# A spill store moved from ScalarE's program to SyncE's, in an attention stage that transposes its probabilities through HBM

## The chip, the core and the metric

The program runs on one core of one Trainium2 chip. The metric is the device time of one execution, in microseconds (us). The profiled execution is looked at through its span, from the first to the last instruction. PE is TensorE, PEld its weight loads, DVE is VectorE, ACT is ScalarE, POOL is GpSimd, SP is SyncE, which only issues DMAs here.

## The reference

Four layers follow one another on 2 x 1024 tokens of 256 features: attention with 16 heads of 128, a gated MLP, attention with 16 heads of 16, and a mixture of experts. The change lies in the first attention:

```python
q = x @ wq + bq; k = x @ wk + bk; v = x @ wv + bv          # weights are codes * scales
scores = einsum('bqhd,bkhd->bhqk', q, k) / sqrt(128)       # 2 batches, 16 heads, 1024 x 1024
attn = softmax(scores, axis=-1)
out = einsum('bhqk,bkhd->bqhd', attn, v).reshape(B, S, 2048)
return out @ wo + bo
```

## The kernel before

The first attention (attention0_stage) works in 8 passes of two heads each, numbered m = 0 to 7. A pass has 32 tiles (TILES): 2 batches x 2 heads x 8 tiles of 128 queries, each against all 1024 keys. Passes 1 to 6 are one hardware loop. Four tiles make a group (GT = 4), so a pass has 8 groups, numbered 0 to 7, with tiles 0 to 3 in group 0. Products are made in three passes of split float32 (line 81).

One tile goes through these steps:

- PE: score(m, tile), 6 matmuls into two of four PSUM banks. It waits until the exponential of tile - 2 is done.
- DVE: row_max (line 1060), the negated maximum of each row.
- ACT: exp (line 934) into one of two buffers prob. It waits for the maximum, and for the turned tile - 2.
- DVE: turn_prob (line 1066), a 32 x 32 block transpose into one of two buffers turned_prob. It waits until the store of tile - 2 has landed (the semaphores stored, four of them in turn).
- A store (line 940) of 512 KB to one of 8 slots of spill in HBM. ACT issues it once the tile is turned.
- A fetch (line 666) of 512 KB back into probT_lo, with 1 KB pieces that complete the transpose. SP issues it once the store has landed. The first fetch of a group also waits until group - 2 has been weighed, since there are two group buffers.
- ACT: probT_take (line 948), the high half. For the first tile of a group it waits for all four fetches of the group.
- POOL: split_lo (line 582), the low half.
- PE: weigh, 6 matmuls with v; then every group's result goes through wo (output) and is added up by DVE.

Each engine walks through slots, one per tile. In slot t PE makes the scores of tile t + 1, then a projection or output, then weighs tile t - 7. DVE in slot t turns tile t, takes the maximum of tile t + 1, then takes projections and outputs out of PSUM, in this order. ACT in slot t takes the high half of tile t - 6, a projection, issues the store of tile t and makes the exponential of tile t + 1:

```python
                if unit is not None and there(m, unit, QK):
                    take_qk(m, unit)
                if there(m, at, TILES):
                    store(m, at)
                if there(m, at + 1, TILES):
                    exp(m, at + 1)
```

SP runs exchange(m): for each group four fetches, and after some groups the loads of the next pass's weights (LOAD_AFTER: after group 0 the q weights and the biases, eight DMAs in lines 617, 621, 634 and 636; after group 1 k, after group 2 v, after group 5 o, five DMAs each). In pass 0, after group 1, set_acc (line 642) comes before the k weights: eight DMAs of 128 KB that each copy the one row bo to all partitions. In pass 7 no weights are loaded; after group 4 SP loads x again (2 x 512 KB) and the first weights of the MLP (lines 1165 to 1170).

DMAs of SP are queue q1 of the profile, those of ACT are queue q10.

Of the kernel before, what the change touches and what calls it, by code (L numbers as in the profile page):

```python
# [20 lines left out]
GT = NB // P  # L21
# [383 lines left out]
def attention0_stage(nc, k, name, ins, after, mlp):  # L405
# [8 lines left out]
    TILES, GROUPS, PARTS = BATCH * half_tiles, BATCH * half_tiles // GT, BATCH * half_tiles  # L414
# [21 lines left out]
    def there(m, i, per_pass):  # L436

        return not isinstance(m, int) or 0 <= m * per_pass + i < passes * per_pass

    def wait(eng, sem, m, per_pass, count):  # L440

        value = m * per_pass + count
        if not isinstance(value, int) or value > 0:
            eng.wait_ge(sem, value)
# [60 lines left out]
    with ExitStack() as ctx:  # L505
# [105 lines left out]
        def _(sp):  # L611
# [32 lines left out]
            def next_weights(m, what):  # L644
# [12 lines left out]
                else:  # L657
                    wait(sp, wo_ready, m, 2, 2)
                    load_wo(m + 1, landed_o)

            def fetch(m, tile):
                group = m * GROUPS + tile // GT
                if tile % GT == 0:
                    wait(sp, weighed, group - 1, GT, 0)
                sp.wait_ge(stored[tile % STORES], (group + 1) * 16)
                sp.dma_start(probT_lo[:, tile // GT % 2, :, tile % GT, :, :].bitcast(F32).rearrange("p a k n -> p a (k n)"),
                             spill[tile % SLOTS].rearrange("(a i) (b n) -> (i b) a n", a=NSQ, b=NSQ)).then_inc(fetched[tile // GT % 2], 16)

            def exchange(m):
                for group in range(GROUPS):  # L670
                    tiles = range(group * GT, (group + 1) * GT)
                    for t in tiles:
                        fetch(m, t)
                    if first(m) and group == 1:
                        for g in range(QG, norm.groups):
                            set_acc(g)
                    if not last(m) and group in LOAD_AFTER:
                        next_weights(m, LOAD_AFTER[group])
                    if last(m) and group == 4:
                        sp.wait_ge(wo_ready, 2 * passes)  # L680
                        for g in range(after.ahead):
                            after.load_x(sp, g)
                        mlp.load_first(sp)
                        mlp.load_second(sp)
# [236 lines left out]
        @block.scalar  # L921
        def _(act):
            def take_qk(m, unit):
                b, head, which, c = qk_part(m, unit)
                wait(act, qk_full, m, QK, unit + 1)
                to = (q, key)[which][0][:, head, c * NB:(c + 1) * NB]
                nc.scalar.activation(to, ring_bank(m, "qk", unit), ACT.Identity,
                                     bias=bias_qk[:, which * HP + head:which * HP + head + 1]).then_inc(qk_hi_done, 1)

            def exp(m, tile):  # L930
                wait(act, max_ready, m, TILES, tile + 1)
                wait(act, turned, m, TILES, tile - 1)
                by_key = scores(tile).rearrange("p a (n b) -> p b (a n)", b=NSQ)
                nc.scalar.activation(prob[:, tile % 2, :].rearrange("p (b n) -> p b n", b=NSQ), by_key, ACT.Exp,  # L934
                                     bias=neg_max[:, tile % 2:tile % 2 + 1],
                                     accum_out=total[:, tile % half_tiles:tile % half_tiles + 1]).then_inc(exp_done, 1)

            def store(m, tile):
                wait(act, turned, m, TILES, tile + 1)
                act.dma_start(spill[tile % SLOTS], turned_prob[:, tile % 2, :]).then_inc(stored[tile % STORES], 16)  # L940

            def probT_take(m, part):
                group, j = part // GT, part % GT
                if j == 0:
                    wait(act, fetched[group % 2], m, 16 * TILES // 2, 16 * GT * (group // 2 + 1))
                wait(act, weighed, m, PARTS, part - GT + 1)
                hi, lo = part_pair(part)
                nc.scalar.activation(hi, f32(lo), ACT.Copy).then_inc(hi_done, 1)  # L948

            def keep_o(m, group):  # L950
                wait(act, weighed, m, PARTS, (group + 1) * GT)
                wait(act, out_full, m, OUTS, 2 * group)
                nc.scalar.activation(o[0][:], o_bank(group), ACT.Copy).then_inc(o_hi_done, 1)

            def v_hi(m, piece):
                half, head = piece // 4, piece // 2 % 2
                wait(act, v_taken, m, V, 4 * half + 2 * (piece % 2 + 1))
                wait(act, weighed, m, PARTS, 16 * half - 8 * (1 - head))
                to, cols = v_piece(piece)
                nc.scalar.activation(v[0][:, to, cols], v_whole[:, to, cols], ACT.Copy).then_inc(v_hi_done, 1)  # L960

            def weights(m, at):
                if not last(m):
                    if at in QK_HI:
                        head = QK_HI[at]
                        wait(act, multiplied, m, 4, 2 if head == 0 else 3)
                        wait(act, qk_full, m, QK, 8 + 4 * (head + 1))
                        nc.scalar.activation(by_row(w[0][:, 0:2, :, head_cols(head)]), by_row(qk_codes[:, :, :, head_cols(head)]),
                                             ACT.Copy).then_inc(w_hi_done, 1)
                    if at == V_HI:  # L970
                        wait(act, multiplied, m, 4, 3)
                        wait(act, v_full, m, V, V)
                        nc.scalar.activation(flat(w[0])[:, 2 * nq:WQKV], codes[:, 2 * nq:WQKV], ACT.Copy).then_inc(w_hi_done, 1)
                if not first(m) and at in WO_HI:
                    head = WO_HI[at]
                    wait(act, multiplied, m, 4, 0)
                    wait(act, out_full, m, OUTS, 0 if head else -4)
                    nc.scalar.activation(wo[0][:, head, :], codes[:, wo_cols(head)], ACT.Copy).then_inc(wo_hi_done, 1)

            def slot(m, at):  # L980
                part = at + 1 - WEIGH_AT
                if there(m, part, PARTS):
                    probT_take(m, part)
                if (at - KEEP_AT) % GT == 0 and there(m, (at - KEEP_AT) // GT, GROUPS):
                    keep_o(m, (at - KEEP_AT) // GT)
                if first(m) and at in TAKE_AT:
                    g = TAKE_AT[at]
                    act.wait_ge(norm.turned, g + 1)
                    norm.take_hi(act, g, turn_banks(g))
                unit = qk_unit(at)  # L990
                if unit is not None and there(m, unit, QK):
                    take_qk(m, unit)
                if there(m, at, TILES):
                    store(m, at)
                if there(m, at + 1, TILES):
                    exp(m, at + 1)
                piece = v_split_at(m, at)
                if piece is not None and there(m, piece, V_PIECES):
                    v_hi(m, piece)
                if at < TILES:  # L1000
                    weights(m, at)
                if last(m):
                    if at in NORM_ACC:
                        after.early_scalar(act, NORM_ACC[at])
                    if at in NORM_X:
                        after.normalise_x(act, NORM_X[at])
                    if at == FIRST_HI:
                        nc.scalar.activation(neg_max[:, 0:1], neg_max[:, 0:1], ACT.Silu)
                        mlp.first_hi(act, first_scaled, first_hi)
                    if at in TAKE_X:  # L1010
                        g = TAKE_X[at]
                        act.wait_ge(after.turned, g + 1)
                        after.take_hi(act, g, last_turn_banks(g))

            for g in range(QG):
                norm.normalise_x(act, g)
            for g in range(QG):
                norm.take_turned(act, g)
            for unit in range(4):
                take_qk(0, unit)  # L1020
                if unit == 1:
                    for g in range(QG, norm.groups):
                        norm.normalise_x(act, g)
            each_slot(act, slot)
# [1645 lines left out]
```

## Time and profile before

| | |
|---|---|
| three runs | 2025.73, 2030.62, 2036.57 us |
| median | 2030.62 us |
| the profiled execution's own time | 2030.62 us |
| its span | 2028.9 us |
| mean granted TensorE clock | 0.97 |
| PE busy over the span | 1906.4 us (94%) |
| PE weight loads, DVE, ACT, POOL busy | 1500.5, 1444.7, 1180.0, 1150.0 us |
| last instruction of the first attention, about | 1157 us |

Busy times of engines overlap, so they don't add up to the span. Each time in a timeline is the start of an instruction from the span's start. The time to landing of a DMA runs from its issue to its completion. A wait is put down to what ended it. Idle time of an engine that is not the bottleneck costs nothing.

### The profile page before, as it was taken

The page shows a single profiled execution, that of the slowest core. Times are in us where ns is not written, and L with a number is a line of the kernel's source. Part 1 is how long each engine was busy: PE and PEld are TensorE (multiplying, and loading weights), DVE is VectorE, ACT ScalarE, POOL GpSimd, SP SyncE. Part 2 cuts the span into 40 slices and gives each one's busy share as a digit, 9 for nine tenths or more (in the row PEclk, how much of TensorE's full clock was granted, in tenths as well). Part 3 has the DMA queues.
Part 4 walks back from the last instruction along what each step waited for, and adds up shares of the span by engine and source line. Part 5 has one row for each costly group of instructions (what it writes and reads, how often), then busy time and mean ns, then how long its engine had stood idle before and what let it go on. Part 6 is the DMA issues. An engine that isn't in the chain of part 4 may idle for free. (4 is left out here: it accounts for less than half of the span.)

```text
span 2028.9 us, 31398 instructions
## 1 busy us (share of the span) xinstructions
PE 1906.4 (94%) x10632; PEld 1500.5 (74%) x10632; DVE 1444.7 (71%) x2367; ACT 1180.0 (58%) x1939; POOL 1150.0 (57%) x856
## 2 busy tenths in 40 slices
PE   6899999999999999999998799899999898999996
PEld 4688888888888888888887587645554457788885
DVE  5678878888788878888888654587677736455555
ACT  4566666666666666666666554377667654333333
POOL 2576776777767767777666562134343435344443
PEclk8899999999999999999999899999999979899998
DMA  7877877878778777787778310000000010110001
GB/s 157 266 249 262 289 258 257 272 261 275 249 257 289 257 254 271 264 269 250 263 254 279 114 43 1 9 7 4 4 4 1 1 56 24 32 32 24 16 1 42
DMA packets 211794, 310.29 MB, mean 153 GB/s; under 512 B 16368, under 2 KB 174832, under 8 KB 211696
## 3 DMA queue, kind: packets, MB, share of 16 engines
q1 hardware_dynamic: 174832, 174.77, 29.7%
q10 hardware_dynamic: 36864, 134.23, 16.4%
q8 instruction: 59, 0.97, 0.2%
q14 instruction: 39, 0.32, 0.1%
HBM read 172.64 MB, written 136.31 MB: 152 GB/s over the span
## 5 line engine op out<-in xcount | busy, mean ns | idle before, releaser
L582 POOL TENSOR_TENSOR attn_probT_lo<-attn_probT_lo,attn_probT_hi 128x1024 fp32r<-128x1024 f32 x254 | 609.7, 2402 | 198.5 <-ACT attn_probT_hi L948 197.9
L1066 DVE STREAM_TRANSPOSE attn_turned_prob<-attn_prob 128x1024 f32<-128x1024 f32 x256 | 318.0, 1242 | 108.0 <-ACT attn_prob L934 58.9
L934 ACT ACTIVATE attn_prob<-psum,attn_neg_max 128x1024 f32<-128x1024 f32 x256 | 285.5, 1115 | 145.9 <-DVE attn_neg_max L1060 143.7
L1060 DVE TENSOR_REDUCE attn_neg_max<-psum 128x1 f32<-128x1024 f32 x256 | 305.7, 1194 | 30.9 <-PE psum L81 30.9
L948 ACT ACTIVATE attn_probT_hi<-attn_probT_lo 128x1024 fp32r<-128x1024 f32 x256 | 269.5, 1053 | 22.8 <-DMA attn_probT_lo<-attn_spill 22.8
L81 PE MATMUL psum<-attn_probT_hi,attn_v_hi 128*128 128x512 f32 x512 | 209.2, 409 | 20.4 <-POOL attn_probT_lo L582 18.7
L81 PE MATMUL psum<-attn_key_hi,attn_q_hi 128*128 128x512 f32 x512 | 204.3, 399 | 7.1 <-ACT attn_prob L934 3.9
L81 PE MATMUL psum<-attn_probT_hi,attn_v_lo 128*128 128x512 f32 x512 | 207.2, 405 | 0.0
L81 PE MATMUL psum<-attn_probT_lo,attn_v_hi 128*128 128x512 f32 x512 | 206.0, 402 | 0.0
L81 PE MATMUL psum<-attn_key_hi,attn_q_lo 128*128 128x512 f32 x512 | 203.2, 397 | 0.0
L2425 ACT ACTIVATE attn_probT<-psum 128x512 f32<-128x512 f32 (+3 forms) x384 | 163.1, 495 | 66.6 <-PE psum L2310 60.0
L81 PE MATMUL psum<-attn_key_lo,attn_q_hi 128*128 128x512 f32 x512 | 200.6, 392 | 0.0
L1624 POOL TENSOR_TENSOR attn_qk_lo<-attn_moe_hidden,attn_qk_hi 128x512 fp32r<-128x512 f32 x72 | 94.3, 1310 | 182.4 <-ACT attn_qk_hi L1588 182.4
L1988 DVE TENSOR_REDUCE attn_peaks<-psum 128x1 f32<-128x512 f32 (+1 forms) x256 | 155.9, 651 | 39.8 <-PE psum L1959 26.3
L785 POOL TENSOR_TENSOR attn_v_lo<-attn_v_whole,attn_v_hi 128x512 fp32r<-128x512 f32 x64 | 83.1, 1299 | 127.9 <-ACT attn_v_hi L960 127.9
L1651 DVE TENSOR_TENSOR attn_moe_hidden<-psum,attn_v 128x512 f32<-128x512 f32 x72 | 49.7, 690 | 137.6 <-ACT attn_v L1582 103.9
L81 PEld LDWEIGHTS psum<-attn_probT_hi,attn_v_hi 128*128 128x128 f32 x512 | 96.9, 189 | 44.1 <-POOL attn_probT_lo L582 12.4
L81 PE MATMUL psum<-xT_hi,attn_q 128*128 128x512 f32 x288 | 119.6, 415 | 6.6 <-POOL attn_key L1620 6.5
L81 PE MATMUL psum<-xT_hi,attn_w_hi 128*128 128x512 f32 x288 | 116.5, 405 | 6.6 <-POOL attn_bias_v L726 5.6
L81 PEld LDWEIGHTS psum<-attn_key_hi,attn_q_hi 128*128 128x128 f32 x512 | 96.8, 189 | 31.8 <-ACT attn_prob L934 5.2
L81 PE MATMUL psum<-xT_hi,attn_key 128*128 128x512 f32 x288 | 117.6, 408 | 0.0
L1588 ACT ACTIVATE attn_qk_hi<-attn_moe_hidden 128x512 fp32r<-128x512 f32 x72 | 45.5, 633 | 123.9 <-DVE attn_moe_hidden L1651 123.9
(237 smaller groups left out, 4782.3 us busy)
## 6 DMA issues: line engine op xcount, KB each, us to landing
attn_spill<-attn_turned_prob ACTq DMA_DIRECT2D x256, 512.0 KB, 3.9
attn_probT_lo<-attn_spill SPq DMA_DIRECT2D x256, 512.0 KB, 5.4
attn_v_all<-in_moe_w SPq DMA_DIRECT2D x23, 384.0 KB, 3.0
acc_sb<-in_x SPq DMA_DIRECT2D x4, 512.0 KB, 7.7
x_sb<-in_wq_codes SPq DMA_DIRECT2D x8, 256.0 KB, 3.9
x_sb<-in_wq_scales SPq DMA_DIRECT2D x32, 64.0 KB, 4.0
x_sb<-in_wk_codes SPq DMA_DIRECT2D x8, 256.0 KB, 4.2
x_sb<-in_wk_scales SPq DMA_DIRECT2D x32, 64.0 KB, 4.9
```

The lines of the kernel that those rows point to most:

```text
L81: ins = nc.tensor.matmul(out, stationary[s], moving[m], start=start and n == 0, stop=stop and n == len(PASSES) - 1)
L582: engine.tensor_tensor(lo, f32(lo), f32(hi), ALU.subtract).then_inc(done, 1)
L785: nc.gpsimd.tensor_tensor(v[1][:, to, cols], v_whole[:, to, cols], f32(v[0][:, to, cols]), ALU.subtract).then_inc(v_done, 1)
L934: nc.scalar.activation(prob[:, tile % 2, :].rearrange("p (b n) -> p b n", b=NSQ), by_key, ACT.Exp, bias=neg_max[:, tile % 2:tile % 2 + 1], ...
L948: nc.scalar.activation(hi, f32(lo), ACT.Copy).then_inc(hi_done, 1)
L1060: nc.vector.tensor_reduce(neg_max[:, tile % 2:tile % 2 + 1], scores(tile), AX.XY, ALU.max, negate=True).then_inc(max_ready, 1)
L1066: nc.vector.transpose(turned_prob[:, tile % 2, :], prob[:, tile % 2, :]).then_inc(turned, 1)
L1588: self.nc.scalar.activation(self.hid[0][p % 2], self.hidden[p % 2], ACT.Copy).then_inc(self.hi_done, 1)
L1624: self.nc.gpsimd.tensor_tensor(self.hid[1][p % 2], self.hidden[p % 2], f32(self.hid[0][p % 2]), ALU.subtract).then_inc(self.lo_done, 1)
L1651: self.nc.vector.tensor_tensor(self.hidden[p % 2], self.k.psum[:, self.slots[p % 2][1], :], self.gate_act[p % 2], ALU.mult).then_inc(self. ...
L1988: nc.vector.tensor_reduce(to[:, h:h + 1], bank[:, 0:width], AX.X, ALU.max, negate=True).then_inc(max_free, 1)
L2425: nc.scalar.activation(probT[:, slot(g, h), q0:], score_bank(g * HG + h)[:, q0:], ACT.Exp, scale=float(D1) ** -0.5).then_inc(exp_done, 1)
```

## The change

The store's issue moves from ACT's program into SP's. SP issues it in exchange, between the fetches: in each group first the stores of tiles 0, 1 and 2, then the fetches of tiles 0 and 1, the store of tile 3 and the fetches of tiles 2 and 3. The new store waits for the same turned tile. It also waits, at the first tile of a group, for the fetches of the group two before, whose slots it overwrites. The weight loads keep their place after the group's last fetch, and thus stand before the next group's stores. ACT no longer waits for the turned tile in its store.

```diff
+            def store(m, tile):
+                group = m * GROUPS + tile // GT
+                if tile % GT == 0:
+                    wait(sp, fetched[tile // GT % 2], m, 16 * TILES // 2, 16 * GT * (tile // GT // 2))
+                sp.wait_ge(turned, group * GT + (tile % GT + 1))
+                sp.dma_start(spill[tile % SLOTS], turned_prob[:, tile % 2, :]).then_inc(stored[tile % STORES], 16)
+
             def fetch(m, tile):
...
             def exchange(m):
                 for group in range(GROUPS):
                     tiles = range(group * GT, (group + 1) * GT)
-                    for t in tiles:
+                    for t in tiles[:3]:
+                        store(m, t)
+                    for t in tiles[:2]:
+                        fetch(m, t)
+                    store(m, tiles[3])
+                    for t in tiles[2:]:
                         fetch(m, t)
                     if first(m) and group == 1:
...
-            def store(m, tile):
-                wait(act, turned, m, TILES, tile + 1)
-                act.dma_start(spill[tile % SLOTS], turned_prob[:, tile % 2, :]).then_inc(stored[tile % STORES], 16)
-
...
-                if there(m, at, TILES):
-                    store(m, at)
                 if there(m, at + 1, TILES):
                     exp(m, at + 1)
```

## Rows read from the trace of the kernel before

**Rows 1.** Busy time of each engine in stretches; granted clock, DMA share, GB/s last.
```profile
core 0: us, PE busy (x) PEld busy (x) DVE busy (x) ACT busy (x) POOL busy (x), PEclk, DMA share, GB/s
20.00:100.00 80.00, 67.33 (x282) 53.37 (x283) 54.49 (x75) 40.97 (x64) 37.80 (x27) 0.86 0.79 209
400.00:600.00 200.00, 199.44 (x994) 166.61 (x994) 162.24 (x201) 133.15 (x197) 145.68 (x81) 1.00 0.77 260
1090.00:1120.00 30.00, 23.70 (x106) 18.23 (x105) 26.56 (x47) 18.56 (x28) 20.69 (x14) 1.00 0.77 275
```

**Rows 2.** The waits from 0 to 1160 us: total, times, longest.
```profile
DVE attn_turned_prob L1066 <- DMA attn_spill<-attn_turned_prob: 48.9, 33, 5.7
```

**Rows 3.** The page, part 3: queue, packets, MB, share of 16 engines' span.
```profile
q1 hardware_dynamic: 174832, 174.77, 29.7%
q10 hardware_dynamic: 36864, 134.23, 16.4%
```

**Rows 4.** SP's queue from 593 to 616 us, pass 4: start, duration, instruction.
```profile
596.37 9.05 SPq L666 DMA_DIRECT2D attn_probT_lo<-attn_spill  x4
...
609.71 0.41 SPq L636 DMA_DIRECT2D attn_bias_v_in<-in_bv  x1
```

**Rows 5.** ACT's stores (line 940) issued at 594.9, 598.4 and 607.1 us.
```profile
DMA to landing us min/median/max: 2.6/2.6/2.6
...
DMA to landing us min/median/max: 6.6/6.6/6.6
...
DMA to landing us min/median/max: 5.7/5.7/5.7
```

**Rows 6.** Timelines of DVE, ACT and PE in the same stretch.
```profile
609.61 1.25 DVE L1066 STREAM_TRANSPOSE attn_turned_prob<-attn_prob 128x1024 f32<-128x1024 f32 x1 [0.58 <-ACT attn_prob L934]
...
612.34 1.11 ACT L934 ACTIVATE attn_prob<-psum,attn_neg_max 128x1024 f32<-128x1024 f32 x1
...
616.52 0.39 PE L81 MATMUL psum<-attn_key_hi,attn_q_hi 128*128 128x512 f32 x1
```

**Rows 7.** SP's queue from 64 to 100 us, pass 0.
```profile
71.19 6.02 SPq L642 DMA_DIRECT2D acc_sb<-in_bo  x8
...
78.42 2.92 SPq L621 DMA_DIRECT2D x_sb<-in_wk_scales  x4
81.44 12.98 SPq L666 DMA_DIRECT2D attn_probT_lo<-attn_spill  x4
```

**Rows 8.** Line 642 from 70 us, line 621 from 77 us, line 940 from 73 us.
```profile
DMA to landing us min/median/max: 5.5/9.4/14.6
...
DMA to landing us min/median/max: 12.2/12.8/13.2
...
L940 ACTq DMA_DIRECT2D attn_spill<-attn_turned_prob x2: 326/326/326, 73.9 to 77.8; - x2
...
DMA to landing us min/median/max: 11.3/12.2/13.2
```

**Rows 9.** Timelines of DVE, ACT and PE, pass 0, slots 10 to 14.
```profile
76.30 1.25 DVE L1066 STREAM_TRANSPOSE attn_turned_prob<-attn_prob 128x1024 f32<-128x1024 f32 x1 [1.27 <-ACT attn_prob L934]
...
82.23 0.39 PE L81 MATMUL psum<-attn_key_hi,attn_q_hi 128*128 128x512 f32 x1
...
88.91 0.50 PE L81 MATMUL psum<-attn_key_hi,attn_q_hi 128*128 128x512 f32 x1 [2.31 <-ACT attn_prob L934]
...
99.45 0.63 PE L81 MATMUL psum<-attn_key_hi,attn_q_hi 128*128 128x512 f32 x1
```

**Rows 10.** A stretch of pass 0, columns as in rows 1.
```profile
92.00:96.00 4.00, 2.14 (x10) 1.84 (x9) 3.38 (x6) 2.15 (x3) 1.77 (x3) 0.50 1.07 369
```

**Rows 11.** Timelines of SP, DVE and PE near the stage's end, pass 7.
```profile
1082.83 0.93 SPq L1170 DMA_DIRECT2D x_sb<-in_ffn_w  x1
...
1088.61 1.25 DVE L1066 STREAM_TRANSPOSE attn_turned_prob<-attn_prob 128x1024 f32<-128x1024 f32 x1 [1.87 <-DMA attn_spill<-attn_turned_prob]
...
1090.02 0.39 PE L81 MATMUL psum<-attn_key_hi,attn_q_hi 128*128 128x512 f32 x1
```

## The prediction

> **What bounds the kernel now.** I read busy time by stretches first, then the waits, then the queues and timelines where the change acts. The edited stage is the first 1158 us of the span. In the middle of it PE is busy 199.44 of 200 us at a granted clock of 1.00 [rows 1]; matmul follows matmul, and no engine that gets faster can shorten this part. PE idles only at the two ends: 12.7 us between 20 and 100 us, where the mean granted clock is also down to 0.86, and 6.3 us between 1090 and 1120 us. So the change can give little and can take more, if it makes something late enough for PE to see. The loop that it touches runs beside PE: DVE takes a tile's maximum, ACT the exponential, DVE turns it, a DMA stores it, a DMA fetches it back. DVE may turn tile t only when store t-2 has landed, and it waits 48.9 us for that in 33 places [rows 2], nearly all hidden under PE.
>
> **What stays the same in bytes.** From the shares of the two queues [rows 3] a fetch holds the 16 engines 0.297 x 2028.9 x 512 / 174832 = 1.76 us (512 packets) and a store 0.164 x 2028.9 / 256 = 1.30 us. Both stay; only who issues them, and so what is ahead of them, changes.
>
> **ACT's part: nothing.** ACT loses 256 issues of 0.33 us and its wait for the turned tile. Its next exponential waits for the maximum, which DVE takes only after turning the same tile, so the issue lies under that 1.19 us reduction. Credit: 0.
>
> **The new order in a group: a small gain, hidden.** A store issued at 594.9 us alone lands in 2.6 us; the one of 598.4 us, behind three fetches issued from 596.37 us on, takes 6.6 us [rows 4, 5]: 3 x 1.76 + 1.30 = 6.6, so data goes nearly in order of issue although the store sat on another queue. With two fetches ahead it lands 1.76 us earlier, at 603.3 instead of 605.0 us, and the fourth fetch goes out that much sooner. PE is full there, so this is worth 0; it only cushions what follows. The Trainium skill, DMA: Bandwidth & Descriptors, section "Queues, rings and completion order", says each DMA engine takes turns between the queues packet by packet. By that rule the store of 598.4 us should have had every other packet and landed some 2 x 1.30 + 1.3 = 3.9 us after its issue (an estimate); the 6.6 us disagree.
>
> **Stores behind the weight loads: the price.** After groups 0, 1, 2 and 5 SP issues the next pass's weights. Today ACT stores meanwhile; afterwards the first stores of the next group stand behind these issues in SP's program and in its queue, DVE's turn of tile t+2 stands behind the landing, and behind that on DVE the next maximum and the q, k, v and output takes; ACT and then PE's scores follow.
>
> Steady passes, worst after group 0 (eight DMAs). The fourth fetch is issued at 605.06 and the last load ends at 610.12 us [rows 4], 5.06 us later; from 603.3 us that gives 608.4 us for store 4, against about 604 now. It then lands after 2.6 us if nothing is ahead, after 5.7 us if it fares like the store issued amid these loads [rows 5]: 611.0 to 614.1 us. I take 612.2, nearer the lower end, because most loads are 2 us old by then. DVE's turn of tile 6 moves from 609.61 to 612.3 us, +2.7. From that turn's start to the end of exp 7 is 612.34 + 1.31 - 609.61 = 4.0 us (1.11 us and 0.2 for the read of the accumulator that follows). PE starts score 9, which needs exp 7, at 616.52 us [rows 6], 2.9 us after that end. At +2.7 PE loses nothing; at the upper end +4.6 it loses 1.7 us per pass. With jitter I take 0.2 us for each of 7 passes, 1.5 in all; the bounds are 0 and 12. The five-DMA loads after groups 1, 2 and 5 take 2 us less to issue: 0.
>
> Pass 0, after group 1: here set_acc's eight loads (6.02 us of issue from 71.19 us) and the k weights (until 81.3 us) come before tile 8's store [rows 7]. These set_acc loads are slow: up to 14.6 us from issue to landing; the k scales behind them, the last issued at about 80.8 us, take 12.2 us or more, so they land at 93.0 us, and ACT's two stores of 73.9 and 77.8 us suffer too, 11.3 and 13.2 us [rows 8]. Store 8, issued at 70.8 us now, will be issued at 81.4 us. It lands no later than 93.0 + 1.3 = 94.3 us and, with the two stores of 1.30 us gone from ahead, no earlier than 91.7; I take 92. DVE turns tile 10 at 92.1 instead of 76.30 us. By the 4.0 us above, exp 11 ends at 96.1 us, and PE's score 13, at 82.23 us now, starts at 96.2, 14.0 us late. Part of it is lost today as well, because stores 9 and 10 hold up DVE: score 14 at 88.91 after 2.31 us idle, score 15 at 99.45 us, with the clock at 0.50 in between [rows 9, 10]. Unhindered at full clock these two slots take 4.4 us (82.23 to 88.91 less the idle time) and 5.0 (half of the 10.5 us from 88.91 to 99.45, mostly at the lower level). So score 15 comes at 96.2 + 9.4 = 105.6 us, 6.2 us later than now. PE is idle for these 14.0 us before, and today it fell to the lower of its two levels (1.2 GHz) after shorter idleness; coming back at that level for 4 to 10 us costs 2 to 5 us more. I take 3.3: pass 0 costs 9.5 us, with bounds 5 and 12. The four scores or more between here and the next loads have slack again, so nothing adds up.
>
> **The end of the stage.** In pass 7 no weights are loaded, but after group 4 SP issues six loads (1.9 MB) that end at 1083.8 us [rows 11], say 1082 with the earlier fetch. They hold the engines about 6 us (q1 moves 174.77 MB in 603 us), so store 20 lands at about 1088 us, tile 22 is turned at 1088 instead of 1083, and tile 23, by the same 4.0 us, at 1092.2 instead of 1088.61 us. Score 25, at 1090.02 us, moves to 1092.2. PE idles after this anyway, waiting on this chain: +2 us, bounds 0 and 4.
>
> **Sum.** 9.5 + 1.5 + 2 = 13 us on a profiled time of 2030.62 us (span 2028.9, 1.7 around it), which is also the median of the three runs: 2043.6 us.
>
> **Rivals.** (1) The delay shows in every pass: stores after the q load fare like the one of 607.1 us. Then 12 instead of 1.5 us: 2054, and more if the clock dips. For it: 5.7 us was measured; the bias loads read one row for all partitions, as set_acc does. Against it: 2.9 us of slack and a shorter backlog. (2) Nothing measurable: pass 0's stall mostly replaces today's, and the end gains as much as it loses. Pass 0 at its lower bound 5, no steady loss, end -1: 2035. That the queue does not matter speaks for it; that store 8 can't be issued before 81.3 us speaks against it. The Trainium skill, same page, section "Issuing engines are not separate DMA queues", says that issuing from several engines saves only issue time. By it alone, one would expect about no change; the rows on order of issue agree that the queue itself is nearly neutral, but the place in SP's program is not. (3) Faster: store 3 ahead of the third fetch makes every group's last fetch 1.8 us earlier, and at the two ends, where PE idles about 25 us in all, half of that goes: 2019. It decides only if store 8 lands before about 78.5 us (76.30 plus the 2.2 us by which exp 11 is early for score 13), thus if set_acc's loads were not ahead of it; they are, in program order.
>
> **How the numbers follow.** Main case 0.55 (2036 to 2050), rival 1 0.17, rival 2 0.20, rival 3 0.08. About 0.5%, 10 us, is what a measurement of this kernel can tell from no change; the bound for slower is thus 2040.8 us. Above it lie two thirds of the main case and rival 1: slower 0.54; faster 0.08; within 0.5% 0.38. The range leaves out rival 3 and the far side of rival 1: 2031 to 2058.
>
> **What would show it.** DVE's turn of pass 0 waits some 15 us once for a store near 77 to 92 us; PE has its longest idle time there, about 14 us, and a stretch at half clock after it. In a middle pass the fourth fetch lands 1.8 us earlier, store 4 is issued at the end of SP's loads, DVE waits about 2 us for it, and PE stays full. If PE idles after every q load, rival 1 holds; if tile 8's store lands before 85 us, my reading of pass 0 is wrong.

## The result, and the profile after

| | before | after |
|---|---|---|
| median of four runs | 2029.05 us | 2057.17 us |
| lowest to highest | 2025.73 to 2036.57 | 2054.74 to 2060.03 |
| the profiled execution's own time | 2030.62 us | 2058.2 us |
| its span | 2028.9 us | 2056.5 us |

The ratio is 1.0134 with an interval of 1.0102 to 1.0167: the change makes the kernel 28 us slower. In the changed kernel the store is line 666 in SP's queue, the fetch line 673, the exponential line 946, the row maximum 1066 and the turn 1072.

Parts 1 and 3 of the page of the kernel after. All DMAs of the stage are now in q1; no queue of ACT is left:
```profile
PE 1913.6 (93%) x10632; PEld 1497.0 (73%) x10632; DVE 1438.9 (70%) x2367; ACT 1178.0 (57%) x1939; POOL 1149.5 (56%) x856
...
q1 hardware_dynamic: 211696, 309.00, 45.3%
q8 instruction: 59, 0.97, 0.2%
```

Its busy time by stretches, columns as in [rows 1]:
```profile
20.00:100.00 80.00, 57.61 (x247) 44.58 (x247) 47.00 (x58) 38.23 (x60) 31.30 (x23) 0.87 0.76 192
92.00:96.00 4.00, 2.48 (x6) 2.00 (x7) 3.38 (x5) 2.75 (x5) 1.50 (x1) 0.50 0.99 278
96.00:100.00 4.00, 4.00 (x17) 3.20 (x16) 3.33 (x4) 3.22 (x5) 2.75 (x2) 0.88 0.97 360
400.00:600.00 200.00, 197.92 (x972) 164.55 (x971) 159.03 (x197) 129.47 (x193) 146.00 (x83) 0.99 0.76 258
1090.00:1120.00 30.00, 26.04 (x121) 20.79 (x119) 18.45 (x23) 14.51 (x22) 13.86 (x7) 0.96 0.77 246
```

Against [rows 1], PE lost 9.7 us of work between 20 and 100 us (67.33 to 57.61), and 1.5 us in the 200 us in the middle, which was full before. The last row doesn't compare one to one with the last of [rows 1]: at 1090 us the kernel after is some 23 us behind, so it is doing there what the kernel before did from 1067 us on.

The waits from 0 to 1160 us (total, times, longest):
```profile
DVE attn_turned_prob L1072 <- DMA attn_spill<-attn_turned_prob: 120.2, 43, 17.1
...
PE psum L81 <- ACT attn_prob L946: 23.5, 9, 13.5
```

DVE's wait for stores went from 48.9 us [rows 2] to 120.2 us, and one of them lasts 17.1 us.

To see where the 27.6 us of span went, the start of PE's last score matmul of tile 0 is compared pass by pass. The first and the last of these rows in the kernel after, and then in the kernel before:
```profile
177.54 0.39 PE L81 MATMUL psum<-attn_key_hi,attn_q_lo 128*128 128x512 f32 x1
...
1008.08 0.39 PE L81 MATMUL psum<-attn_key_hi,attn_q_lo 128*128 128x512 f32 x1
```
```profile
172.71 0.39 PE L81 MATMUL psum<-attn_key_hi,attn_q_lo 128*128 128x512 f32 x1
...
984.87 0.39 PE L81 MATMUL psum<-attn_key_hi,attn_q_lo 128*128 128x512 f32 x1
```

Passes 1 to 6 take 1008.08 - 177.54 = 830.5 us instead of 984.87 - 172.71 = 812.2. The whole account, with the experiments told below beside it, is in the table: what each kernel's profiled execution loses against that of the kernel before, in us, up to the score of tile 4 of pass 0 (start), from there to tile 0 of pass 1 (pass 0), from there to tile 0 of pass 7 (passes 1 to 6), and on to tile 31 of pass 7. A minus means time gained.

| kernel | start | pass 0 | passes 1 to 6 | pass 7 | sum |
|---|---|---|---|---|---|
| after | -3.2 | 8.0 | 18.4 | 5.2 | 28.4 |
| late_all | -3.0 | 11.5 | 46.5 | 3.2 | 58.2 |
| late_pass0 | -1.9 | 9.9 | 15.2 | 4.6 | 27.8 |
| late_steady | -3.0 | 6.1 | 43.7 | 6.2 | 53.0 |
| late_qk | -2.2 | 7.7 | 47.6 | 4.2 | 57.4 |
| act_first | -4.6 | 3.5 | -1.1 | 1.4 | -0.8 |
| after_acc | -2.5 | 0.7 | 11.3 | 5.7 | 15.2 |
| before_acc | -1.9 | -6.9 | 1.2 | -0.4 | -8.0 |
| v_later | -2.8 | 7.2 | 10.2 | 4.5 | 19.1 |
| inwait_acc | -3.0 | 0.3 | 9.8 | 3.9 | 11.0 |
| act_first_acc | -2.9 | -6.9 | -0.5 | 1.8 | -8.5 |
| ahead | -3.0 | 2.5 | -0.7 | 2.1 | 0.9 |
| ahead_acc | -4.1 | -3.7 | -0.9 | 2.1 | -6.7 |

The start is 2 to 5 us shorter in every other kernel than in that one execution of before, before_acc with its old stores among them; PE waited 5.61 us there for POOL's bias_v, and 2.57 in the kernel after. No edit reaches this part, so I take it for that execution's own.

Each row is one execution, and the table covers the first attention alone. The span of ahead's execution, say, is 9.3 us above that of before, and 8.4 of these lie behind the stage. Passes 1 to 6 also spread: after, late_pass0 and after_acc run the same code there and lose 18.4, 15.2 and 11.3 us. So a difference of a few us between two cells of that column proves nothing. The steps from about 0 (act_first, ahead) to 11 and more, and to over 40 (the late kernels), are clear of this spread.

Idle time alone would understate the loss. Between the two score matmuls above, PE is shown busy for 820.35 of 830.54 us, and for 811.60 of 812.16 in the kernel before: 9.6 us more idle time, and 8.8 us more busy time for the same matmuls, among them longer ones right behind the waits (0.50 instead of 0.39 us at 786.00 us below). A short stretch at the lower clock is part of it: in pass 3 PE is busy for 1.92 of the 4 us from 506 us on, and from 510 to 514 us the granted clock is 0.58.

**One steady pass.** SP's queue in pass 5 of the kernel after, around its q, k and v loads:
```profile
751.41 5.57 SPq L673 DMA_DIRECT2D attn_probT_lo<-attn_spill  x2
757.27 0.38 SPq L617 DMA_DIRECT2D x_sb<-in_wq_codes  x1
...
760.79 0.38 SPq L636 DMA_DIRECT2D attn_bias_v_in<-in_bv  x1
761.31 5.44 SPq L666 DMA_DIRECT2D attn_spill<-attn_turned_prob  x3
...
775.33 0.45 SPq L617 DMA_DIRECT2D x_sb<-in_wk_codes  x1
...
777.97 5.99 SPq L666 DMA_DIRECT2D attn_spill<-attn_turned_prob  x3
...
795.03 0.83 SPq L666 DMA_DIRECT2D attn_spill<-attn_turned_prob  x2
```

The store of tile 4 is issued at 761.31 us, right behind the last q load; the stores of tiles 8 and 12 likewise follow the k and v loads, at 777.97 and 795.03 us. Their landing times, in this order; each view holds two stores, and the lowest time is that of the one named:
```profile
DMA to landing us min/median/max: 3.8/4.2/4.6
...
DMA to landing us min/median/max: 4.4/4.8/5.1
...
DMA to landing us min/median/max: 5.9/6.3/6.7
```

DVE's turns of tiles 6, 10 and 14 wait for them:
```profile
765.16 1.25 DVE L1072 STREAM_TRANSPOSE attn_turned_prob<-attn_prob 128x1024 f32<-128x1024 f32 x1 [3.04 <-DMA attn_spill<-attn_turned_prob]
...
782.36 1.25 DVE L1072 STREAM_TRANSPOSE attn_turned_prob<-attn_prob 128x1024 f32<-128x1024 f32 x1 [3.11 <-DMA attn_spill<-attn_turned_prob]
...
800.94 1.25 DVE L1072 STREAM_TRANSPOSE attn_turned_prob<-attn_prob 128x1024 f32<-128x1024 f32 x1 [3.89 <-DMA attn_spill<-attn_turned_prob]
```

and PE, from 783 to 805 us:
```profile
786.00 0.50 PE L81 MATMUL psum<-attn_key_hi,attn_q_hi 128*128 128x512 f32 x1 [0.25 <-ACT attn_prob L946]
...
804.00 0.39 PE L81 MATMUL psum<-attn_w_hi,xT_hi 128*128 128x256 f32 x1 [1.62 <-DVE attn_q_lo L1050]
```

Each wait is 3 to 4 us. The first costs PE nothing, but leaves score 9 with 0.74 us to spare, where it had 2.9 [rows 6]. The second arrives before that has grown back: score 12 has 2.0 us to spare in each steady pass, where it has 3.4 in the kernel called ahead, below; at 786.00 us score 13 already waits 0.25 us. The third then shows as 1.62 us idle at 804.00 us, where a projection waits for DVE's q_lo, which stands in DVE's program behind the late turn.

One delay of the same size costs nothing. The o load stands by itself, after group 5; the turn of tile 26 behind it waits 2.8 to 3.8 us in each steady pass, in pass 5:
```profile
851.66 1.25 DVE L1072 STREAM_TRANSPOSE attn_turned_prob<-attn_prob 128x1024 f32<-128x1024 f32 x1 [2.81 <-DMA attn_spill<-attn_turned_prob]
```

PE loses nothing by it in five of the six passes, and 0.7 us in pass 1.

**Pass 0.** SP's queue, DVE's turn of tile 10 and PE, in the kernel after:
```profile
69.72 5.43 SPq L642 DMA_DIRECT2D acc_sb<-in_bo  x8
75.19 1.55 SPq L617 DMA_DIRECT2D x_sb<-in_wk_codes  x1
76.80 6.66 SPq L621 DMA_DIRECT2D x_sb<-in_wk_scales  x4
83.94 7.52 SPq L666 DMA_DIRECT2D attn_spill<-attn_turned_prob  x3
```
```profile
89.88 1.25 DVE L1072 STREAM_TRANSPOSE attn_turned_prob<-attn_prob 128x1024 f32<-128x1024 f32 x1 [17.05 <-DMA attn_spill<-attn_turned_prob]
```
```profile
93.52 0.79 PE L81 MATMUL psum<-attn_key_hi,attn_q_hi 128*128 128x512 f32 x1 [13.49 <-ACT attn_prob L946]
...
104.35 0.39 PE L81 MATMUL psum<-attn_key_hi,attn_q_hi 128*128 128x512 f32 x1
```

The four scale loads of k took 6.66 us to issue instead of 2.92 [rows 7], with set_acc's eight copies (up to 13.2 us to landing) still under way. The store of tile 8 goes out at 83.94 us, DVE waits 17.05 us and PE 13.49 us, and the granted clock is 0.50 between 92 and 96 us. From 96 to 100 us it is back at 0.88, while in the kernel before it was still 0.50 there.

**The end.** DVE and PE near the end of the stage, in the kernel after:
```profile
1113.70 1.25 DVE L1072 STREAM_TRANSPOSE attn_turned_prob<-attn_prob 128x1024 f32<-128x1024 f32 x1 [7.96 <-DMA attn_spill<-attn_turned_prob]
```
```profile
1117.35 0.64 PE L81 MATMUL psum<-attn_key_hi,attn_q_hi 128*128 128x512 f32 x1 [3.96 <-ACT attn_prob L946]
```

The store of tile 20 is issued at 1105.56 us, right after the six loads, and lands 8.0 us later; tile 22 waits 7.96 us for it, PE then 3.96 us. Behind this idle time the granted clock is 0.69 from 1116 to 1120 and 0.50 from 1120 to 1124 us, so score 26 is 7.4 us later than in the kernel before, where score 25 was 4.1 us later (both without the 23.2 us lost up to there).

### The profile page after: what moved, and what is told of

It reads as the page before. It is cut to its first block and busy times, and to the rows that moved or that the text cites. A ratio compares the mean times of both kernels' runs of the same rounds, so it can differ in the third digit from the quotient of the medians.

```text
span 2056.5 us, 31580 instructions
## 1 busy us (share of the span) xinstructions
PE 1913.6 (93%) x10632; PEld 1497.0 (73%) x10632; DVE 1438.9 (70%) x2367; ACT 1178.0 (57%) x1939; POOL 1149.5 (56%) x856
## 5 line engine op out<-in xcount | busy, mean ns | idle before, releaser
L1072 DVE STREAM_TRANSPOSE attn_turned_prob<-attn_prob 128x1024 f32<-128x1024 f32 x256 | 318.1, 1243 | 193.5 <-DMA attn_spill<-attn_turned_prob 120.2
L946 ACT ACTIVATE attn_prob<-psum,attn_neg_max 128x1024 f32<-128x1024 f32 x256 | 285.7, 1116 | 243.4 <-DVE attn_neg_max L1066 242.1
L81 PE MATMUL psum<-xT_lo,attn_q 128*128 128x512 f32 x288 | 117.3, 407 | 0.0
```

The source lines that it names most:

```text
L81: ins = nc.tensor.matmul(out, stationary[s], moving[m], start=start and n == 0, stop=stop and n == len(PASSES) - 1)
L1072: nc.vector.transpose(turned_prob[:, tile % 2, :], prob[:, tile % 2, :]).then_inc(turned, 1)
```

## The experiments

Two theories stood at first. The theory of the place: the first store of a group is late because SP must first issue the loads, whatever the queue. The theory of the queue: stores suffer because they share q1 with fetches and loads.

**late_all, late_pass0, late_steady, late_qk: the loads behind the next group's stores.** `others` is set_acc, the weight loads and pass 7's six loads, moved as they are.

```diff
                     for t in tiles[:3]:
                         store(m, t)
+                    if group and late(m, group - 1):
+                        others(m, group - 1)
                     for t in tiles[:2]:
                         fetch(m, t)
...
+                    if not late(m, group):
+                        others(m, group)
```

late is true always in late_all, in pass 0 alone in late_pass0, in passes 1 to 6 in late_steady, and in late_qk in passes 1 to 6 for groups 0 and 1.

> The changed kernel, but set_acc, every weight load and the six loads of pass 7 are issued after the first three stores of the next group instead of before them. Theory 1, the place in SP's program: DVE's waits for a store fall from 120 us to under 55, PE is full from 130 to 1090 us, pass 0 loses at most 3 us, and the time is 2025 to 2035 us, within 0.5% of the kernel before. Theory 2, the shared queue: a store on SP's queue fares worse wherever it stands, so at least half of the 28 us stays: 2045 us or more.

> The changed kernel with only pass 0's loads and set_acc moved behind the first three stores of the next group. Theory 1: the 13.9 us idle time of PE in pass 0 goes and 8 us come back (less 2 us, since the slow copies then delay the fetches), the steady 18 us and the end's 5 us stay: about 2050 us. Theory 2: nothing comes back: 2057 us. If pass 0's cost was only moved, the same.

> The changed kernel with only the loads of passes 1 to 6 moved. Theory 1: the 18 us that passes 1 to 6 lose come back, pass 0's 8 us and the end's 5 us stay: about 2039 us. Theory 2: 2057 us.

> The changed kernel with only the q and k loads of passes 1 to 6 moved; the v loads, after which PE idles in each pass, stay in place. Theory 1a, lateness adds up over three loads (2.7, 2.7 and 4.1 us of DVE waits against 2 to 3 us of slack): the v load alone is hidden, PE loses under 0.7 us per pass, 2040 us. Theory 1b, the v load alone does it: PE still loses about 3 us per pass near tiles 12 to 17, 2057 us.

Measured, beside before at 2024.89 us: late_all 2089.43 us, ratio 1.0307 (1.0267 to 1.0347); late_pass0 2062.18, 1.0166 (1.0125 to 1.0206); late_steady 2082.86, 1.0272 (1.0240 to 1.0304); late_qk 2096.21, 1.0350 (1.0305 to 1.0395). None recovers the loss, and where steady passes are touched it more than doubles. Moving the q and k loads alone costs the steady passes as much as moving all four (47.6 and 46.5 us). SP's queue in late_all:
```profile
787.32 0.39 SPq L617 DMA_DIRECT2D x_sb<-in_wq_codes  x1
...
791.01 0.38 SPq L636 DMA_DIRECT2D attn_bias_v_in<-in_bv  x1
791.53 0.93 SPq L673 DMA_DIRECT2D attn_probT_lo<-attn_spill  x2
792.58 0.45 SPq L666 DMA_DIRECT2D attn_spill<-attn_turned_prob  x1
793.07 7.72 SPq L673 DMA_DIRECT2D attn_probT_lo<-attn_spill  x2
800.99 1.13 SPq L666 DMA_DIRECT2D attn_spill<-attn_turned_prob  x2
```

The q load now stands in group 1. There the first two fetches (tiles 4 and 5) are late, issued at 791.53 us behind the loads, and the store of tile 7 at 792.58 is behind their data: it lands after 7.8 us. The fourth fetch must wait for this landing, and in SP's program the next group's first store, of tile 8, stands behind that wait, at 800.99 us. The loads had been moved, not the wait. So SP's order has two such places, and stores can be held up at either. The theory of the place was wrong in its detail, and the theory of the queue is not told apart by these four.

**act_first: only each group's first store goes back to ACT.** Shortened, against the kernel after:

```diff
-                    for t in tiles[:3]:
+                    for t in tiles[1:3]:
                         store(m, t)
...
+                if at % GT == 0 and there(m, at, TILES):
+                    store(m, at)
                 if there(m, at + 1, TILES):
                     exp(m, at + 1)
```

The wait for the earlier fetches stands at the group's second tile instead of its first.

> The changed kernel, but ACT issues the store of the first tile of each group again, 64 per pass-half, a quarter of all stores; SP issues the other three. Theory 1, SP's program is one line of waits: only a group's first store stands behind the wait of the fourth fetch and the loads, so the 18 us of passes 1 to 6 come back, and most of the end's 5; pass 0 keeps most of its loss, since store 9 stays behind set_acc. About 2037 us. Theory 2, the shared queue: a quarter of the loss comes back at most, 2050 us.

Measured 2031.13 us, before 2028.38, ratio 1.0009 (0.9989 to 1.0029), less than the 2037 us expected. Three quarters of the stores are still SP's, and nothing is lost. Its busy time in the middle, and DVE's waits for stores from 100 to 1110 us (92.9 us in the kernel after, 38.2 before):
```profile
400.00:600.00 200.00, 200.00 (x998) 167.17 (x997) 164.34 (x203) 133.63 (x199) 145.23 (x82) 1.00 0.76 262
```
```profile
DVE attn_turned_prob L1078 <- DMA attn_spill<-attn_turned_prob: 10.4, 11, 3.6
```

PE is full again. The store behind the loads was the whole of the steady loss (-1.1 us are left in passes 1 to 6); but this store also changed its queue, so the two theories are told apart only by the run called ahead, below.

**after_acc, before_acc: set_acc's later copies made on the chip.** Tiles of the second half copy rows that are already there, instead of reading the one row bo from HBM for 128 partitions, in the kernel after and in the kernel before.

```diff
+                if g == QG:
+                    sp.wait_ge(acc_set, 16 * QG * GT)
                 for t in norm.tiles(g):
-                    sp.dma_start(k.acc[:, t, :], ins["bo"].partition_broadcast(P)).then_inc(acc_set, 16)
+                    rows = ins["bo"].partition_broadcast(P) if g < QG else k.acc[:, t - QG * GT, :]
+                    sp.dma_start(k.acc[:, t, :], rows).then_inc(acc_set, 16)
```

> The changed kernel, but the second half of set_acc copies from the accumulators that the first half has set, on chip, instead of reading one HBM row for all partitions; the same number and size of DMAs at the same place. Theory 1 says that the slow landing of these eight, not their issue time, makes most of pass 0's idle time: tile 8's store lands at about 85 instead of 89.8 us, PE idles about 6 instead of 13.9 us there, 6 to 8 us come back, 2050 us. If the issue time on SP counts instead, nothing comes back.

> The kernel before with the same on-chip copies. Stores 9 and 10 then land 4 us after their issue instead of 11 and 13 us, the two idle times of PE of 2.7 and 2.3 us go, and with them the stretch at half clock: 5 to 9 us faster than before. If these copies are not what slows the stores, no change.

Measured: after_acc 2047.66 us, 1.0092 (1.0064 to 1.0120); before_acc 2024.20, 0.9973 (0.9953 to 0.9993). The eight copies land in 2.6 to 5.3 us in before_acc, instead of 5.5 to 14.6 [rows 8]. DVE and PE in pass 0 of after_acc:
```profile
82.36 1.25 DVE L1075 STREAM_TRANSPOSE attn_turned_prob<-attn_prob 128x1024 f32<-128x1024 f32 x1 [10.18 <-DMA attn_spill<-attn_turned_prob]
```
```profile
86.01 0.79 PE L81 MATMUL psum<-attn_key_hi,attn_q_hi 128*128 128x512 f32 x1 [6.63 <-ACT attn_prob L949]
```

The idle time falls from 13.49 to 6.63 us, and pass 0's loss from 8.0 to 0.7. The issue of the eight copies still takes 5.65 us, but that of the k scales falls from 6.66 to 1.91, and the store goes out at 78.20 instead of 83.94 us. So about half of pass 0's stall was these copies' slowness, the other half the order of issue. This doesn't make half of the price theirs: the kernel before gains as much from quick copies (6.9 us in pass 0, before_acc). With quick copies on both sides the new order costs 0.7 + 6.9 = 7.6 us there, with slow ones 8.0.

**v_later: the v load one group later.** This breaks up the row of three.

```diff
-    LOAD_AFTER = {0: "q", 1: "k", 2: "v", 5: "o"}
+    LOAD_AFTER = {0: "q", 1: "k", 3: "v", 5: "o"}
```

> The changed kernel with the v load after group 3 instead of group 2. Theory 1a, DVE's lateness adds up over three loads in a row and recovers in a group without one: PE's loss of about 3 us per pass falls to 1 us or less, 2045 us. Theory 1b, the v load does it by itself: the loss stays, four tiles later, 2057 us.

Measured 2050.21 us, 1.0108 (1.0073 to 1.0144). Passes 1 to 6 lose 10.2 instead of 18.4 us, 1.7 per pass, where 1 or less was expected if the delays only add up. As after_acc, with v in its old place, lost 11.3, the sum alone shows little; where the time goes shows more. Below, the loss of passes 1 to 6 by the scores before which it arises (time from the last score matmul of one tile to that of the next, less the same time in the kernel before, added up over the six passes). Scores 13 and 14 follow the delay by the k load, 17 and 18 that by the v load in its old place; the last column has all 32 scores:

| kernel | scores 10 to 12 | 13 and 14 | 17 and 18 | all |
|---|---|---|---|---|
| after | 1.7 | 11.8 | 5.2 | 18.4 |
| late_pass0 | 3.5 | 8.0 | 3.1 | 15.2 |
| after_acc | 0.9 | 7.6 | 3.2 | 11.3 |
| v_later | 2.0 | 8.5 | 0.0 | 10.2 |
| ahead | 0.0 | 0.4 | 0.0 | -0.7 |

The loss of the v load (3.1 to 5.2 us) is gone in v_later, and none arises at its new place, scores 21 and 22 (0.0); the turn of tile 18 waits 0.6 to 1.5 us there. The larger part of the steady loss, at scores 13 and 14, stays with two loads in a row. No run has the k load without the q load ahead of it. How much of this part is the slack that the q load took can be estimated only: score 12 had 1.4 us less to spare (3.4 less 2.0), which is at most some 8 us in six passes. The k load's own waits (2.9 to 4.9 us in after) reach above 2.9 us in five of six passes, so part may be its own.

**inwait_acc: the loads ahead of the fourth fetch,** where SP may wait for the store of tile 3 anyway; with set_acc as in after_acc.

```diff
-                    for t in tiles[2:]:
-                        fetch(m, t)
+                    fetch(m, tiles[2])
+                    others(m, group)
+                    fetch(m, tiles[3])
```

> All stores on SP as in the changed kernel, set_acc's second half copied on chip, and every load issued between a group's third and fourth fetch, where SP otherwise stands 4.8 us waiting for the store of tile 3. Theory 1: the loads fill that wait, the next group's first store goes out 0.5 to 1 us after it is turned, and passes 1 to 6 lose nothing or up to 1 us each, because the fourth fetch now has the loads' data ahead of it: 2028 to 2036 us. Theory 2, the shared queue and its data: as after_acc, 2048 us. If the fourth fetch is made too late, ACT's high halves wait for it and PE for POOL's low halves.

Measured 2043.45 us, before 2030.15, ratio 1.0055 (1.0030 to 1.0081). Against after_acc the steady loss is nearly the same (9.8 and 11.3 us). In pass 5 the next group's first store is issued earlier, at 744.06 us, 1.0 us after the last load began, but it lands only 7.7 us later: now the loads' and the fetch's data is ahead of it. What is saved in SP's program is paid in the queue. The expected 2028 to 2036 us were missed: a store can be late by its place in the program or by the data issued just ahead of it.

**act_first_acc:** act_first with set_acc's copies on the chip.

```diff
+                if at % GT == 0 and there(m, at, TILES):
+                    store(m, at)
...
+                    rows = ins["bo"].partition_broadcast(P) if g < QG else k.acc[:, t - QG * GT, :]
```

> ACT issues each group's first store, SP the other three, and set_acc's second half is copied on chip: the two best parts together. Pass 0 loses its 10 us idle time of PE near 92 us as well; PE is full from 100 to 1090 us: 6 to 10 us faster than the kernel before, about 2020 us, and the same as the kernel before with the copies alone within 3 us. If the two cures overlap, it is no faster than act_first.

Measured 2027.21 us, 0.9983 (0.9954 to 1.0011). Pass 0 gains 6.9 us, as in before_acc, but the whole kernel only 3 us where 6 to 10 were expected; the interval still holds 1.

**ahead, ahead_acc: every store by SP, but the next group's first store ahead of the last fetch and the loads.** ahead_acc also has set_acc's copies on the chip.

```diff
+                if first(m):
+                    store(m, 0)
                 for group in range(GROUPS):
...
-                    for t in tiles[:3]:
+                    for t in tiles[1:3]:
                         store(m, t)
...
-                    for t in tiles[2:]:
-                        fetch(m, t)
+                    fetch(m, tiles[2])
+                    if not last(m) or group < GROUPS - 1:
+                        store(m, tiles[3] + 1)
+                    fetch(m, tiles[3])
```

> All stores stay on SP and on its queue, the loads stay where the change left them, but SP issues the first store of the next group before the last fetch of this one, thus before the loads. The next tile is turned about 4.3 us after tile 3, and that fetch waits 4.8 us for tile 3's store, so it costs the fetch nothing. Theory 1, the place in SP's program: passes 1 to 6 lose under 0.5 us each, pass 0 keeps a loss of some 4 us (store 9 stays behind set_acc), about 2031 us, as with ACT issuing that store. Theory 2, sharing one queue costs in itself: passes 1 to 6 still lose more than half of their 18 us, 2045 us or more.

> The same with set_acc's second half copied on chip. Theory 1: pass 0's loss goes too, and the time is 2018 to 2026 us, faster than the kernel before and within 3 us of act_first_acc and before_acc. If the order of SP's program were not the cause, it stays above 2035 us.

Measured, before at 2027.88 us: ahead 2029.82, ratio 1.0000 (0.9974 to 1.0026); ahead_acc 2021.96, 0.9962 (0.9936 to 0.9988). ahead_acc and before_acc are the only kernels whose intervals lie below 1, and these overlap: the gain is that of the copies, with either engine's stores. SP's queue of ahead around the q load, the middle stretch, and DVE's waits for stores from 100 to 1110 us:
```profile
736.69 0.33 SPq L666 DMA_DIRECT2D attn_spill<-attn_turned_prob  x1
737.30 0.36 SPq L673 DMA_DIRECT2D attn_probT_lo<-attn_spill  x1
737.94 0.51 SPq L617 DMA_DIRECT2D x_sb<-in_wq_codes  x1
...
741.63 0.38 SPq L636 DMA_DIRECT2D attn_bias_v_in<-in_bv  x1
742.12 0.36 SPq L666 DMA_DIRECT2D attn_spill<-attn_turned_prob  x1
```
```profile
400.00:600.00 200.00, 200.00 (x998) 167.17 (x997) 163.51 (x203) 133.80 (x199) 145.69 (x81) 1.00 0.76 260
```
```profile
DVE attn_turned_prob L1076 <- DMA attn_spill<-attn_turned_prob: 7.7, 6, 2.7
```

Store 4 goes out at 736.69 us, before the last fetch and the eight loads; the next store follows at 742.12. PE is busy for 200.00 of 200 us, and DVE waits 7.7 us in all instead of 92.9. Every DMA is still in q1. That decides for the theory of the place: ACT's queue is not needed, only a different order of SP's instructions. Pass 0 and the end still lose 2.5 and 2.1 us.

## Why the prediction was right in direction and too low in size

The time fell into the range, near its upper end (2058), and slower was the likeliest case. The point, 2043.6 us, was 13.6 us too low, and the main case (2036 to 2050) doesn't hold the result. The range reached it only through rival 1, and not for rival 1's reason; that part is luck. By its own steps:

- **ACT's part, nothing; the new order in a group, hidden.** Both right. In the waits from 100 to 1110 us, ACT's wait for fetches fell from 22.5 us before to 1.0 after, and PE got nothing from it. The best that moving the stores gave by itself is ahead, at 1.0000.
- **Steady passes, 1.5 us with bounds 0 and 12: measured 18.4, above the upper bound.** This is the term that was mis-sized; in the other two executions with the same steady code it was 15.2 and 11.3. The reading of the q load was close: issued at the end of the loads, as said, landing in 3.8 us (taken: 3.8, from 608.4 to 612.2), DVE's wait 3.04 (predicted: about 2, with a turn 2.7 us later). And as said, it costs PE nothing by itself. The step that failed is the next sentence, "The five-DMA loads after groups 1, 2 and 5 take 2 us less to issue: 0." With it fails "so nothing adds up", said of pass 0. The prediction weighed each load against the full slack of 2.9 us. But the groups follow every four slots, and after the q load 0.74 us of the slack is left, after the k load nothing; the k and v loads cost DVE 3.11 and 3.89 us, not less than the q load's 3.04, and PE pays from there: 11.8 us behind the k load, 5.2 behind the v load. For the o load, alone in its place, the 0 held. v_later, which breaks up the row, loses nothing behind the v load any more; act_first and ahead, which take the store out from behind the loads, get all of it.
- **Pass 0, 9.5 us: measured 8.0.** Store 8 was issued at 83.94 instead of 81.4 us, and in an execution that began some 3 us earlier; it landed in 5.8 us where I had taken 10.6, probably because the copies were further along. PE's idle time of 14.0 us came out as 13.49, the turn's wait of "some 15 us" as 17.05, and the stretch at half clock came. Score 15 starts at 104.35 us; 105.6 was forecast. But with the earlier start taken off, two errors cancel in part: score 15 is 8.1 us late, not 6.2, and nothing is lost behind it, where 3.3 were set aside for coming back at the lower clock. That return lay in the two slots behind score 13 (10.8 us instead of 9.4), and so cost some 1.4. after_acc and before_acc add what the prediction didn't ask: with quick copies the same order costs 7.6 us here.
- **The end, +2 us with bounds 0 and 4: measured 5.2, above the upper bound.** Store 20 landed 8.0 us after its issue behind the six loads, where about 6 were taken, and tile 22 waited 7.96 us, where a turn at 1088 instead of 1083 was forecast. Score 25 came 4.1 us late, not 2.2, and the lower clock behind it was not in the sum. With the first store of the group ahead of them, 1.4 and 2.1 us are left.
- **The rivals.** Rival 1, a delay in every pass at 2054 us, gave nearly the measured time, but not for its reason: stores after the q load don't fare like the one of 607.1 us (3.8, not 5.7 us), and PE doesn't idle after the q load. The loss shows in every pass, but behind the k and v loads, where unremarkable delays come in a row. Rival 2, nothing measurable, is what ahead and act_first do, and rival 3 never came about. The Trainium skill, DMA: Bandwidth & Descriptors, section "Issuing engines are not separate DMA queues", says that DMAs share the same engines whoever issues them, and that starting them from several engines only saves the time of issuing. On the queue ahead agrees, at 1.0000. The section adds that this time "is usually small relative to the DMA itself"; here 28 us hung on what a single issuing program had to go through before the store, though each issue took under 1 us in the steady passes.

In numbers: 13 predicted, + 16.9 steady, + 3.2 at the end, - 1.5 in pass 0, - 3.2 at the start, which is no effect of the change, make the 28.4 of the table.

What stays open: how much of the loss at scores 13 and 14 is the slack that the q load took and how much the k load's own delay, and why the same steady code lost between 11.3 and 18.4 us. That late_qk is no faster than late_all, though it moves fewer loads, can be placed: late_qk loses 13.2 us at scores 17 and 18, behind the v load that kept its place, where late_all loses 2.7; late_all loses 7.5 us at scores 19 to 22 and 2.3 before score 10, where late_qk loses none. That the v load in its old place meets the delay of the moved k load there is likely, not shown by a run.

## What to carry to other kernels

An engine that issues DMAs runs its program in order: when a transfer moves to it, look for what stands ahead of it there, loads to be issued and waits for other landings, and put the transfer that someone waits for first. Which queue it goes by can matter far less than this. And when a delay is smaller than the slack it is hidden under, ask how soon the next delay comes and how much of the slack has grown back by then: waits of about 3 us against a slack of 2.9 cost 2 to 3 us per pass here where three of them came four slots apart, and next to nothing where one came by itself.

## What the runs showed of the hardware

- Copying one row of HBM to all 128 partitions was slow here, and what stood behind it was slow too. Eight such copies of 128 KB landed after 5.5 to 14.6 us [rows 8]; the same bytes copied from rows already on the chip after 2.6 to 5.3 us. This edit alone takes 6.9 us out of pass 0 of the kernel before, ratio 0.9973.
- Issuing DMAs took longer behind the slow copies: four scale loads took 6.66 us there, 1.91 us behind the quick ones, and 1.94 us in pass 5 (the q scales at 757.75 us).
- On the single queue a store's time to landing went with what was issued just ahead of it: 3.8 us behind the q load, 7.7 us behind loads and a fetch in inwait_acc, 8.0 us behind the six loads of pass 7.
